# First expert stage of a two-layer vision model in pairs of 64-slot units instead of 128-slot tiles

## What is computed

```
route = softmax(hidden @ router_w + router_b)
max_prob, max_ind = max(route), argmax(route)
for e in range(8):
    oe = silu(x @ w1[e]) * (x @ w2[e]) @ w3[e]
    out += where(max_ind == e, oe, 0)
out = out.astype(bfloat16) * max_prob
```

## Time and profile before

| | |
|---|---|
| runs | 386.35, 388.22, 392.8 us; median 388.22 us |
| the profiled execution | 386.41 us, of which the span is 384.7 us |
| PE busy | 345.8 us (90%) |
| PEld busy | 294.6 us (77%) |
| DVE busy | 190.5 us (50%) |
| ACT busy | 143.2 us (37%) |
| POOL busy | 97.2 us (25%) |
| moved by DMA | 60.44 MB, mean 157 GB/s |

### The profile page before, as it was taken

One profiled execution on the slowest core, in us unless ns is written; L12 is line 12 of the kernel. 1 busy time (PEld: TensorE's weight loads), 2 busy tenths in 40 slices (PEclk: granted clock), 3 DMA queues, 4 the chain that ended last, 5 costly groups with the idle time before them and its releaser, 6 DMA issues.

```text
span 384.7 us, 7223 instructions
## 1 busy us (share of the span) xinstructions
PE 345.8 (90%) x2791; PEld 294.6 (77%) x2801; DVE 190.5 (50%) x515; ACT 143.2 (37%) x290; POOL 97.2 (25%) x128
## 2 busy tenths in 40 slices
PE   5999969789669999999986899878899999999996
PEld 2999935587568999985565475765799999999995
DVE  3786788676642233228696752437321511432125
ACT  3997222953303222233693143331222212212130
POOL 4399606000032443211105002000523232321210
PEclk9999976957986999999997899977999999999999
DMA  7933219991481795035006999020259999999822
GB/s 243 375 78 90 67 54 273 255 256 30 126 225 35 228 241 139 12 91 128 0 3 161 278 219 250 15 68 3 68 121 271 270 260 248 244 252 241 215 62 88
DMA packets 30515, 60.44 MB, mean 157 GB/s; under 512 B 10705, under 2 KB 17106, under 8 KB 30482
## 3 DMA queue, kind: packets, MB, share of 16 engines
q1 hardware_dynamic: 28242, 54.71, 54.5%
q0 software_dynamic: 2240, 5.28, 5.1%
HBM read 55.12 MB, written 4.85 MB: 156 GB/s over the span
## 4 chain that ended last, share of the span: by engine, by line
PE 74%; DVE 14%; ACT 6%; issue 3%; DMA 2%; POOL 1%; DVEq 0%; POOLq 0%
PE ps L1715 16%; PE ps L1740 14%; PE ps L1727 9%; PE ps L1464 8%; PE ps L1523 4%; PE ps L1456 4%; PE ps L1529 3%; DVE cv L1369 2%; DMA xg<-token_x,src_id 2%; PE ps L1658 2%; PE ps L1691 2%; PE ps L1867 1%; PE ps L1914 1%; PE ps L1629 1%; PE ps L1578 1%
## 5 line engine op out<-in xcount | busy, mean ns | idle before, releaser
L1715 PE MATMUL ps<-xgt,wup 128*128 128x128 f32 x576 | 70.7, 279 | 2.0 <-DVE ht L1266 1.6
L1715 PEld LDWEIGHTS ps<-xgt,wup 128*128 128x128 f32 x576 | 69.3, 196 | 2.5 <-issue 2.5
L1266 DVE TENSOR_TENSOR ht<-sg,ps 128x384 f32<-128x384 f32 (+1 forms) x56 | 27.8, 497 | 63.4 <-ACT sg L822 59.7
L618 POOL DMA_INDIRECT xg<-token_x,src_id x26 | 25.3, 972 | 134.0 <-DVE src_id L1236 82.6
L1740 PE MATMUL ps<-wdn,ht 128*128 128x192 f32 x288 | 53.8, 335 | 0.0
L1740 PEld LDWEIGHTS ps<-wdn,ht 128*128 128x128 f32 x288 | 46.1, 190 | 3.2
L822 ACT ACTIVATE sg<-ps 128x384 f32<-128x384 f32 (+1 forms) x56 | 24.9, 445 | 42.6 <-PE ps L1727 41.9
L1727 PE MATMUL ps<-xgt,wup 64*128 64x128 f32 x576 | 40.7, 286 | 0.0
L1464 PE MATMUL ps<-weff,xp 128*128 128x193 f32 x240 | 40.4, 330 | 0.0
L1464 PEld LDWEIGHTS ps<-weff,xp 128*128 128x128 f32 x240 | 39.7, 192 | 0.7 <-DVE weff L943 0.7
L1727 PEld LDWEIGHTS ps<-xgt,wup 64*128 64x128 f32 x576 | 35.3, 191 | 3.8 <-issue 2.5
(11 more groups left out here) (315 smaller groups left out, 528.7 us busy)
## 6 DMA issues: line engine op xcount, KB each, us to landing
wup<-in_m_w SPq DMA_DIRECT2D x16, 576.0 KB
wup<-in_m_w SPq DMA_DIRECT2D x48, 192.0 KB
wdn<-in_m_w SPq DMA_DIRECT2D x16, 576.0 KB
wup<-in_m_w SPq DMA_DIRECT2D x12, 384.0 KB, 4.0
wup<-in_m_w SPq DMA_DIRECT2D x36, 128.0 KB, 4.0
wdn<-in_m_w SPq DMA_DIRECT2D x12, 384.0 KB, 5.7
xw<-in_xw SPq DMA_DIRECT2D x2, 784.0 KB, 10.5
wall<-in_w_sh SPq DMA_DIRECT2D x2, 768.0 KB, 8.9
```

Of the source, the lines that this page charges most:

```text
L618: g.indirect_dma_start(xg[:, j, :], None, token_x[m], bass.IndirectOffsetOnAxis(ap=src_id[:, j:j + 1], axis=0))\
L1266: v.tensor_tensor(ht[:, j % 2, s, 0:half], sg[:, s, 0:half], ps[:, 2 * s + 1, 0:half], ALU.mult)\
L1715: mm(ps[:, 2 * s + g, c * P:c * P + P], up[:, col:col + P], xgt[:, 0, j * P:j * P + P], start=(c == 0), stop=False)
```

## The change

Tiles of the first mixture become pairs of *units* with 64 slots each. There are `M1_HALVES = (576 + 8*63)//64 = 16` units, so 8 pairs (`M1_TILES = 8`) and 16 weight sets, still in 8 buffers; unit j belongs to expert j for j < 8 and to `te[j-8]` after that. A pair's two units have different experts. The operands change places: the 64 slots of a unit are stationary, in one column half of the array (so one unit's results are on partitions 0 to 63 and the other's on 64 to 127), and the expert's weights move, 512 wide. Hidden units now stand along a row of `ht`, so `hidden_across` transposes them (four 128x128 transposes on TensorE, one copy 128x512 from PSUM on DVE) before `down_pair`. The rank arithmetic uses 64 in place of 128. The last four units are kept. Set j from 8 on is loaded when `p_y` says that pair (j-8)//2 is through. A few semaphores elsewhere are merged, with no instruction added.

```diff
-M1_TILES = (T + E * (P - 1)) // P
+H = 64
+M1_HALVES = (T + E * (H - 1)) // H
+M1_TILES = M1_HALVES // 2
...
+        hx = ht[:, :, :, M1_H // 2:M1_H // 2 + P]
...
-        KEPT_AFTER = ((4, 6), (4, 9))
+        KEPT_AFTER = ((2, 3), (4, 9))
...
-                for j in range(first, r["n"]):
+                for j in range(first, M1_HALVES if m == 0 else r["n"]):
                     if j == E:
                         sp.wait_ge(S["v_te"], m + 1)
-                    sp.wait_ge(S["p_y"], j - r["bufs"] + 1 + r["before"])
+                    last = j - r["bufs"]
+                    if last >= 0:
+                        sp.wait_ge(S["p_y"], (last // 2 if m == 0 else last) + 1 + r["before"])
...
+                    gates = ps[:, 2 * s, 0:half]
+                    if m == 0:
+                        gates = ps[:, 2 * (j % 2), s * half:s * half + half]
+                        if j >= 1:
+                            act.wait_ge(S["v_ht"], 2 * (j - 1) + s + 1)
...
+                def hidden_across(j):
+                    dve.wait_ge(S["p_hx"], j + 1)
+                    v.tensor_copy(hx, ps[:, 5, :].rearrange("p (s c n) -> p s c n", s=2, n=P))\
+                        .then_inc(S["v_hx"], 1)
...
+                def up_pair(j):
+                    if j >= 2:
+                        pe.wait_ge(S["v_ht"], 2 * (j - 2) + 2)
+                    for t in (2 * j, 2 * j + 1):
+                        b, uses = weight_uses(0, t)
+                        pe.wait_ge(S[f"d_wb{b}"], 16 * W_LOADS * uses)
...
+                    for g in range(2):
+                        for i in range(2):
+                            at = j * P + H * i
+                            mm(ps[H * i:H * i + H, 2 * (j % 2) + g, :], xgt[:, 0, at:at + H],
+                               wbuf[0][(2 * j + i) % M1_BUFS][0][:, g * hid:(g + 1) * hid], start=True, stop=False)
+                def up_pair_rest(j):
+                    for i in range(2):
+                        for g in range(2):
+                            at, rows = j * P + H * i, slice(REM * g, REM * g + REM)
+                            ins = mm(ps[H * i:H * i + H, 2 * (j % 2) + g, :], xgt[rows, 1, at:at + H],
+                                     wbuf[0][(2 * j + i) % M1_BUFS][0][rows, 2 * hid:3 * hid], start=False, stop=True)
+                    ins.then_inc(S["p_gu"], 2)
+                def hidden_across(j):
+                    pe.wait_ge(S["v_ht"], 2 * j + 2)
...
+                    for c in range(hid // P):
+                        ins = nc.tensor.transpose(ps[:, 5, c * P:c * P + P],
+                                                  ht[:, j % 2, c // 2, c % 2 * P:c % 2 * P + P], ident[:])
+                    ins.then_inc(S["p_hx"], 1)
+                def down_pair(j):
+                    pe.wait_ge(S["v_hx"], j + 1)
...
+                    for c in range(hid // P):
+                        for i in range(2):
+                            ins = mm(ps[H * i:H * i + H, 4, 0:D], hx[:, c // 2, c % 2, H * i:H * i + H],
+                                     wbuf[0][(2 * j + i) % M1_BUFS][1][:, c, :],
+                                     start=(c == 0), stop=(c == hid // P - 1))
+                    ins.then_inc(S["p_y"], 1)
```

More of the change, by code:

```diff
@@ L340, in weight_uses @@
             if m == 1:
-                uses += len(range(b, M1_TILES, M1_BUFS))
+                uses += len(range(b, M1_HALVES, M1_BUFS))
             return b, uses
@@ L821, in silu @@
                     act.wait_ge(S["p_gu"], j * 2 + (s + 1 + 2 * before))
-                    a.activation(sg[:, s, 0:half], ps[:, 2 * s, 0:half], ACT.Silu).then_inc(S["a_sg"], 1)
+                    gates = ps[:, 2 * s, 0:half]
[3 more added lines that the diff above has]
+                            act.wait_ge(S["v_ht"], 2 * (j - 1) + s + 1)
+                    a.activation(sg[:, s, 0:half], gates, ACT.Silu).then_inc(S["a_sg"], 1)
                 def result(j):
@@ L828, in result @@
                         act.wait_ge(d_y[j % 2], j // 2 * 16 + scattered(m))
-                    a.copy(ysb[m][:, j % 2, :], ps[:, 4 + j % 2, 0:D]).then_inc(S["a_y"], 1)
+                    a.copy(ysb[m][:, j % 2, :], ps[:, 4 + (j % 2 if m == 1 else 0), 0:D]).then_inc(S["a_y"], 1)
                 act.wait_ge(S["p_gt"], 2 * GROUPS[m] + 2)
@@ L897, in _ @@
                 a.activation(ysq[:, r, 0:T], yt[:, r, 0:T], ACT.Square).then_inc(S["a_ysq"], 1)
-            a.activation(root[:], eps_t[:], ACT.Sqrt).then_inc(S["a_root"], 1)
+            a.activation(root[:], eps_t[:], ACT.Sqrt)
             act.wait_ge(S["p_ssq"], 1)
@@ L1146, in experts @@
                 r = MOE[m]
-                n, half, before, K = r["n"], r["hid"] // 2, r["before"], r["k"]
+                n, half, before, K, L = r["n"], r["hid"] // 2, r["before"], r["k"], r["slots"]
+                over = (M1_HALVES if m == 0 else n) - E
                 i_ln = 2 if m == 0 else 5
@@ L1249, in experts @@
                     link(v.tensor_tensor(gate[:, 1], gate[:, 0], ex8[:, :, 0], ALU.mult))
[L1251 to L1254, removed]
+                link(v.tensor_tensor(teb[:, 0:over, :], base_e[0:1, 1:E].unsqueeze(1).broadcast_to([1, over, E - 1]),
+                                     iota_t[:, 0:over, :], ALU.is_le))
+                link(v.tensor_reduce(tef[:, 0:over], teb[:, 0:over, :], AX.X, ALU.add))
+                v.tensor_scalar(te[:, 0:over], tef[:, 0:over], float(E - 1), None, ALU.min).then_inc(S["v_te"], 1)
                 def gathered(i):
@@ L1265, in product @@
                     dve.wait_ge(S["a_sg"], j * 2 + (s + 1 + 2 * before))
-                    v.tensor_tensor(ht[:, j % 2, s, 0:half], sg[:, s, 0:half], ps[:, 2 * s + 1, 0:half], ALU.mult)\
+                    ups = ps[:, 2 * s + 1, 0:half]
+                    if m == 0:
+                        ups = ps[:, 2 * (j % 2) + 1, s * half:s * half + half]
+                    v.tensor_tensor(ht[:, j % 2, s, 0:half], sg[:, s, 0:half], ups, ALU.mult)\
                         .then_inc(S["v_ht"], 1)
@@ L1287, in last_units @@
                     v.tensor_tensor(one_last[m][:, l, 0], one_last[m][:, l, 0], one_last[m][:, l, 1], ALU.add)                        .then_inc(S["v_ol"], 1)
+                def hidden_across(j):
+                    dve.wait_ge(S["p_hx"], j + 1)
+                    v.tensor_copy(hx, ps[:, 5, :].rearrange("p (s c n) -> p s c n", s=2, n=P))\
+                        .then_inc(S["v_hx"], 1)
                 for j in range(n):
+                    if m == 0 and j >= 1:
+                        hidden_across(j - 1)
                     if j == 0:
@@ L1304, in experts @@
                         last_units(KEPT_AFTER[m].index(j))
+                if m == 0:
+                    hidden_across(n - 1)
             def routed(t):
@@ new lines, in experts @@
+                if m_ == 0:
+                    for j in range(n):
+                        up_pair(j)
+                        if j >= 1:
+                            hidden_across(j - 1)
+                        if j == 0:
+                            gathered(1)
+                        elif j % 2 == 1 and j + 1 < n:
+                            gathered(j // 2 + 2)
+                        elif j == n - 1:
+                            for l in range(KEPT):
+                                kept_across(l)
+                        up_pair_rest(j)
+                        if j >= 1:
+                            down_pair(j - 1)
+                    hidden_across(n - 1)
+                    down_pair(n - 1)
+                    combine()
+                    return
```

42 lines of the change are left out of this document (27 added, 15 removed).

## The result

| | before | after |
|---|---|---|
| median of 20 runs each | 387.47 us (383.42 to 392.8) | 390.94 us (386.64 to 393.98) |
| ratio, with its 95% interval | | 1.0073 (1.0038 to 1.0108) |
| the profiled execution | 386.41 us, span 384.7 | 393.77 us, span 392.0 |
| PE, PEld busy | 345.8, 294.6 us | 339.7, 264.3 us |
| DVE, ACT, POOL busy | 190.5, 143.2, 97.2 us | 190.8, 137.1, 89.2 us |

A forecast was written before the change was run, and what follows sets the result against it. It took TensorE alone to bound the stage before and weight loads at 247 GB/s after: +5.6 us to combine plus 1.4 for the clock, +7.0 on 388.2, said as 395 us, range 388 to 402 us.

The forecast's parts named there:

- What becomes the bound: First expert stage: weight loads set the pace at 247 GB/s; TensorE waits some 3.7 us a pair from pair 5 on.
- up_pair, hidden_across, down_pair, the copy: Pieces of a pair in the first expert stage: 1.76, 0.64 and 1.51 us on TensorE, DVE's copy 0.69 us.
- up_pair_rest: Second up piece of a pair: two array quarters at a time, 1.76 + 0.20 change-over, 1.96 us.
- When the loads start: Second-round weight loads wait for down_pair(0), ending at 126.9 us; SP issues the first at 128.1 us.
- How long they take: Eight weight sets, one gather and six scatters, 9.87 MB at 247 GB/s: 39.9 us, last landing at 168.0 us.
- The end: From up_pair(7) at 168.1 us through down_pair(7) at 178.0; combine begins at 178.6, +5.6 us.
- The clock in the last pair: After a wait, 1.2 GHz would cost the last pair 2.9 us; half taken, 1.4 us.
- four quarters at a time, loads as reckoned: Rival: up_pair_rest on four quarters, loads starting 1.9 us earlier, last rest 0.88 shorter: 392.4 us, inside the forecast's range.
- The rival on the other side: Weights come in time, TensorE sets the pace: -5.2 us, 383; decided at 287 GB/s; chance 0.08.

The follow-up runs named there:

- the run that forces two at a time: Changed kernel with a one-column full-array matmul between the two units' halves of up_pair_rest: 395.35 us, ratio 1.0192.
- the run with the filled waits: Changed kernel with 18 useless matmuls on TensorE ahead of up_pair(4) to up_pair(7): 390.34 us, ratio 1.0101.
- Columns only: Changed kernel, packed HBM layout, up weights loaded as 1024 and 512 columns, each piece on all 128 partitions: 373.07 us, ratio 0.9644.
- whole rows: Changed kernel with up weights packed in HBM, a set loaded in two 128-partition transfers in place of five: 372.85 us, ratio 0.9669.
- a third of the bytes: Changed kernel, sets 8 to 15 loading only 128 of 1536 up-weight columns and the third weight whole, output wrong: 374.88 us, ratio 0.9713.
- up weights early: Changed kernel with the first two weights of sets 8 to 15 loaded after up_pair_rest, only the third after down_pair: 381.97 us, ratio 0.9887.
- 64 and 64: Changed kernel, packed layout, first 1024 up-weight columns in one piece, last 512 in two pieces of 64 partitions: 385.62 us, ratio 0.9913.

## Why the prediction was wrong in size

It said +7.0 us, and +6.8 at the median; the stage has +3.9, and the ratio +2.8. The sign and the cause held. What failed first is the price of `up_pair_rest`: two quarters of the array at a time, 1.96 us, where the runs show four at once, 1.02.

- **What becomes the bound: right.** Waits for weights, and DMA near 250 GB/s without a break, from 129 to 169 us. The forecast was 3.7 us each ahead of pairs 5, 6 and 7; they are 4.72, 3.68, 2.77 and 1.91, from pair 4 on, since a pair is 5.0 us and not 6.09.
- **up_pair, hidden_across, down_pair, the copy: right.** 1.76, 0.64, 1.51, 0.69 forecast; 1.72, 0.59, 1.45, 0.70 measured. Column halves 512 wide run side by side.
- **up_pair_rest: this step failed.** "Between two at a time (4 x 0.44 = 1.76) and four at a time (0.88) I take 1.76, since all rows show pairs." It is 0.88 + the change-over: 1.02 us (1.91 at half clock), and the run that forces two at a time shows 2 x 1.00 at full clock. The rows showed pairs because the code before used only two tiles at once; that was no evidence on four. It counts three times: at the entry (3.72 forecast, 1.91), in rest(1) (1.96, 1.02), and in the last pair (1.96, 1.02), 3.6 us together. TensorE: Matmul & The Clock Gate in the Trainium skill (Part 3) had it that tiles which are distinct run at once, and this row agrees with it.
- **When the loads start.** 12.3 us after the start of rest(0) was forecast; it is 9.0 (119.09 to 128.11): **-3.3**. Of that, 1.8 and 0.9 are the two rests; the remaining 0.6 is small differences in up_pair(1), down_pair(0) and SP's issue.
- **How long they take: the rate was right, the duration short.** From the first issue to pair 7 39.9 us were forecast (9.87 MB at 247 GB/s); it is 42.7 (128.11 to 170.83), **+2.8**. 9.98 MB moved at a mean of 234: the windows hold 248, 252, 244, 235, and the first two microseconds have little in flight.
- **The end.** From pair 7 to `combine` 10.5 us were forecast, and it is 9.33 (170.83 to 180.16), **-1.2**, 0.9 of it the last rest.
- **The clock in the last pair: wrong.** Half of 2.9 us was put in for a lower clock. The clock fell after the three longer waits (3.68, 3.25 and 2.85 us for `up_pair`) and not after the last, of 1.91 us (1.94): **-1.4**. That the other falls come out of the waits was right, and the run with the filled waits shows it. The half was argued and not read from a row.

7.0 - 3.3 + 2.8 - 1.2 - 1.4 = 3.9, the stage's difference.

The rival "four quarters at a time, loads as reckoned" (392.4) was nearest; the forecast should have stood on it. Part of that nearness is luck: it leaves out the 2.8 us that the loads took longer, starts them only 1.9 us earlier where it was 3.3, and keeps 1.4 for a clock that did not fall. The rival on the other side was put at a rate above 287 GB/s, with a chance of 0.08. For the kernel as it was, that was right. What I had wrong was to take 250 GB/s as a limit of "these loads" and not of how they are cut: slice 2 of the page at 375 GB/s said that more was to be had, and I put it down to wide rows. "Columns only" shows that width was not it. (That no window with expert weights goes above 271 was also a little off: slice 7 of the page has 273 and slice 23 has 278, both with such loads. The argument is untouched.)

## What to carry to other kernels

When a change makes the fast engine faster and brings more bytes, price the bytes' stretch from the first transfer that can start to the last that is waited for; what then counts is the work ahead of that first transfer, and not the work behind waits. Ask of a transfer that fills the DMA engines below the best rate of the same trace how many partitions each piece spans, and lay the data out in HBM so that each piece spans all 128: here this was worth 4% where the loads set the pace; where they didn't, the stage showed nothing of it. That rows show two of something at once tells what the code asked for and not what the array can do.

## What was not expected of the hardware

- Eight float32 instructions 512 wide over four quarters of the array (64 rows by 64 columns each) take 1.02 us, and four of them over two quarters 1.00 us.
- Transfers that fill all sixteen DMA engines (share 1.0 and over) move 232 to 257 GB/s when two thirds of their bytes go in pieces of 96, 64 or 32 partitions, and 362 to 415 when all go in pieces of 128, with packets of 2.7 or 4.1 KB alike.
- SP needs 3.1 us to issue the five transfers of a set, and 1.7 us for a set of two (122.10 to 123.78 with whole rows). With a third of the bytes that alone held pair 5 up by 2.10 us.
- TensorE's granted clock at the entry of the stage is 0.50 in some executions and 1.00 in others, also where nothing that TensorE does ahead of it was changed: 1.5 us of the stage.
- The same stretch behind `combine` lasts between 207.0 (up weights early) and 212.9 us (64 and 64) in the profiled executions, though these edits touch nothing that is computed there. (With a third of the loads, where other values go on, it is 218.9; that execution was 10 us above its kernel's median.) A few microseconds of a single execution say nothing about an edit; the length of the stage does, once the clock at its entry is allowed for.
